# A fused attention and mixture-of-experts layer on one core: a third row buffer, a reordered DMA queue, one group's statistics moved to ScalarE, and three first chunks turned by DMA

## Time and profile before

| | |
|---|---|
| median of 3 runs (lowest, highest) | 440.42 us (439.35, 440.53) |
| the profiled execution | 441.75 us |
| its span, first to last instruction | 440.0 us |
| TensorE busy | 420.4 us, 96% |
| VectorE, ScalarE, GpSimd busy | 322.4, 222.7, 228.3 us |
| chain that ended last | PE 64%, DVE 13%, DMA 11%, issue 4%, ACT 4% |

### The profile page before, as it was taken

How to read it: one execution, slowest core, us unless ns; L and a number is a source line. 1 busy time by engine, 2 the same in 40 slices (tenths; PEclk the granted TensorE clock), 3 DMA queues, 4 the chain that set the end, 5 groups by cost and what they waited for, 6 DMA issues and landing times.

```text
span 440.0 us, 8367 instructions
## 1 busy us (share of the span) xinstructions
PE 420.4 (96%) x3015; PEld 288.6 (66%) x3015; DVE 322.4 (73%) x838; ACT 222.7 (51%) x444; POOL 228.3 (52%) x353
## 2 busy tenths in 40 slices
PE   6899999998999899999989999999999999999996
PEld 2667576756668676766666666666666666665666
DVE  5989778988888478778747787979796967424553
ACT  3755454452657146545424555545455545454551
POOL 3257851826544826056102566575757576757530
PEclk9999999999999999999999999999999999999999
DMA  7996898366945634266866577676888873234840
GB/s 238 294 294 151 277 295 191 74 130 163 279 90 111 139 115 117 57 216 153 120 96 232 165 245 226 205 250 176 281 156 280 179 206 98 90 120 113 159 98 31
DMA packets 104280, 76.01 MB, mean 173 GB/s; under 512 B 73263, under 2 KB 98108, under 8 KB 102192
## 3 DMA queue, kind: packets, MB, share of 16 engines
q1 hardware_dynamic: 92976, 53.11, 47.3%
q0 software_dynamic: 5824, 16.74, 12.9%
q10 hardware_dynamic: 5440, 5.64, 3.9%
HBM read 31.33 MB, written 28.58 MB: 136 GB/s over the span
## 4 chain that ended last, share of the span: by engine, by line
PE 64%; DVE 13%; DMA 11%; issue 4%; ACT 4%; POOL 1%; SPq 1%; another core or an unknown queue 0%; ACTq 0%; POOLq 0%; DVEq 0%
PE bank L1419 18%; PE bank L1421 18%; PE bank L1420 17%; DMA xg<-in_x 4%; DMA pT<-p_rows 3%; PE bank L1510 3%; DVE sc L1012 3%; PE bank L1513 3%; PE bank L1512 3%; PE bank L1491 2%; ACT sc L1269 2%; DVE p_rows L1033 2%; DMA rows<-xg 1%; DMA slots<-xnr,slot_idx 1%; DMA xeT<-slots 1%
## 5 line engine op out<-in xcount | busy, mean ns | idle before, releaser
L1510 PE MATMUL bank<-v_h,pT 128*128 128x257 f16 x272 | 74.7, 274 | 3.2 <-DMA pT<-p_rows 3.2
L1513 PE MATMUL bank<-v_h,pT 128*128 128x257 f16 x272 | 74.1, 272 | 0.0
L1512 PE MATMUL bank<-v_l,pT 128*128 128x256 f16 x272 | 73.7, 271 | 0.0
L1296 ACT ACTIVATE hid_h<-bank 128x512 f16<-128x512 f32 x64 | 38.1, 596 | 67.7 <-PE bank L1421 59.8
L1102 DVE SCALAR_TENSOR_TENSOR hid_l<-bank,hid_h 128x512 f16<-128x512 f32 x64 | 44.0, 688 | 38.0 <-ACT hid_h L1296 33.7
L1421 PE MATMUL bank<-w_h,hid_l 128*128 128x256 f16 x256 | 69.8, 273 | 0.0
L1419 PE MATMUL bank<-w_h,hid_h 128*128 128x256 f16 x256 | 69.8, 273 | 0.0
L1420 PE MATMUL bank<-w_l,hid_h 128*128 128x256 f16 x256 | 69.8, 273 | 0.0
L1012 DVE CUSTOM_DVE_ANT_0 sc<-bank,bias,score_mul 128x512 f32<-128x512 f32 (+2 forms) x80 | 52.9, 664 | 9.1 <-PE bank L1421 9.0
L1419 PE MATMUL bank<-xT,qT_h 128*128 128x512 f16 (+3 forms) x160 | 55.0, 347 | 3.1 <-DVE cmin L1012 1.7
L1285 ACT ACTIVATE pT<-bank 128x512 f16<-128x512 f32 (+3 forms) x50 | 24.6, 494 | 60.3 <-PE bank L1491 50.9
(11 more groups left out here) (198 smaller groups left out, 919.9 us busy)
## 6 DMA issues: line engine op xcount, KB each, us to landing
raw<-in_w_e SPq DMA_DIRECT2D x5, 2048.0 KB
sc<-in_w_e SPq DMA_DIRECT2D x3, 2048.0 KB
slots<-empty ACTq DMA_DIRECT2D x1, 4224.0 KB, 18.7
gates<-gate SPq DMA_DIRECT2D x8, 512.0 KB
out<-xg SPq DMA_DIRECT2D x7, 512.0 KB
rows<-xg SPq DMA_DIRECT2D x7, 512.0 KB, 7.2
rows<-so SPq DMA_DIRECT2D x7, 512.0 KB
xg<-in_x SPq DMA_DIRECT2D x6, 512.0 KB, 4.4
```

What stands on the lines that cost most here:

```text
L1296: a_.activation(hid_h[:, f % HB, :], sc_ps[f % 2][:, :], ACT.Relu).then_inc(h_hi, 1)
L1510: pe.matmul(pv_ps[t % 2][:, 0:D + 1], p_h, v_h[:, at, q, 0:D + 1], start=kb == 0, stop=False)
L1512: pe.matmul(pv_ps[t % 2][:, 0:D], p_h, v_l[:, at, q, :], start=False, stop=False)
L1513: last = pe.matmul(pv_ps[t % 2][:, 0:D + 1], p_l, v_h[:, at, q, 0:D + 1], start=False, stop=kb == t % NT)
```

## The change

- `p_rows` gets a third buffer, which lies in two rows of `hid_h` (used by the experts alone). `pT_in` becomes one semaphore for each tile parity and chunk, and `high` waits for the chunk three DMA turns back.
- `by_dma`: chunk 0 of tiles 15, 27 and 31 is turned by DMA. Before, tile 15 had chunk 1 turned by DMA, 27 and 31 none.
- In the last tile TensorE's turns stand one step later in the order.
- Group 6's RANK stands at step 1 of tile 23 instead of its last step; group 7's VAL units all stand in tile 23 (before: 23 and 24), its PICK and RANK both in tile 24 (before: 24 and 25).
- Group 3's statistics: VectorE's eight instructions and its variance at step 1 of tile 4 go; ScalarE does, for each of the four tiles, a Copy and a Square with accumulated sums, each waiting for the one before it; GpSimd computes the variance with one more instruction.
- SyncE's queue: turn(4) goes behind the chunk_turns of tile 11, two transposes ahead of `top_out(0)` and two behind it. `next_rows(1)` goes behind the chunk_turn of tile 27.

```diff
-        p_rows = [sb(f"p_rows{k}", [P, GT, 2, P], F16) for k in range(2)]
+        p_rows = [sb(f"p_rows{k}", [P, GT, 2, P], F16) for k in range(NX - 1)]
+        p_rows += [hid_h[:, HB - 2:HB, :].rearrange("p f t -> p (f t)").rearrange("p (b h t) -> p b h t", b=GT, h=2)]
...
-            if t in (REST - 1, TILES - 1):
-                return False
+            if t in (NT - 1, REST - 1, TILES - 1):
+                return c == 0
             if chunks(t) == 4:
-                return c == 1 if t == NT - 1 else c in ((1, 2) if t < NT else (0, 1, 2))
+                return c in ((1, 2) if t < NT else (0, 1, 2))
...
-                mine = [PICK] * first + [RANK] * (last and g != NG + 1)
+                mine = [PICK] * first + [RANK] * (c == 1 if g == LATE - 1 else last and g != NG + 1)
...
-                   REST - 5: [VAL, VAL + 1] * last,
-                   REST - 4: [VAL + 2, VAL + 3] * first + [PICK] * (c == 1),
-                   REST - 3: [RANK] * first,
+                   REST - 5: [VAL, VAL + 1] * first + [VAL + 2, VAL + 3] * last,
+                   REST - 4: [PICK] * first + [RANK] * last,
...
-        STATS_TILE = {4: 3, 8: 4, 11: 5, 13: 6, 14: 7}
+        ROOT_TILES = {(4, 1): [0], (5, 0): [1, 2, 3]}
+        STATS_TILE = {8: 4, 11: 5, 13: 6, 14: 7}
...
                 if t == FIRST_SCALE - 1:
-                    spread(0)
+                    turn(NG, range(2))
+                    top_out(0)
+                    turn(NG, range(2, GT))
+                    top_in(0)
...
                     next_rows(0)
-                    next_rows(1)
-
-            spread(1)
+            next_rows(1)
+
+            top_out(1)
+            top_in(1)
...
+                if g == 3:
+                    pool.wait_ge(square3_made, GT)
+                    step(g_.tensor_scalar(var[1][:, :], mv[1][:, :, 1], 1.0 / D, EPS, ALU.mult, ALU.add))
...
-                    if i >= 2:
-                        act.wait_ge(pT_in[i % 2], i // 2 * 16)
+                    if dma_no(t, c) >= NX:
+                        b, m = in_rows[dma_no(t, c) - NX]
+                        act.wait_ge(pT_in[b % 2][m], landed(b, m))
...
+            def statistics(j):
+                act.wait_ge(x_in[1], 32)
+                act.wait_ge(xn_made, made_to(1))
+                act.wait_ge(square3_made, j)
+                a_.activation(unread[:, :], xg[1][:, j, :], ACT.Copy, scale=1.0 / D, accum_out=mv[1][:, j, 0:1]
+                              ).then_inc(mean3_made, 1)
+                act.wait_ge(mean3_made, j + 1)
+                a_.activation(unread[:, :], xg[1][:, j, :], ACT.Square, bias=mv[1][:, j, 0:1], scale=-1.0,
+                              accum_out=mv[1][:, j, 1:2]).then_inc(square3_made, 1)
...
                         high(t, c)
+                    for q in ROOT_TILES.get((t, c), ()):
+                        statistics(q)
...
-                    if c < chunks(t) and not by_dma(t, c):
-                        turn(t, c)
+                    k = c - 1 if t == TILES - 1 else c
+                    if 0 <= k < chunks(t) and not by_dma(t, k):
+                        turn(t, k)
...
+            turn(TILES - 1, chunks(TILES - 1) - 1)
```

More of the change, by code:

```diff
@@ L280, in layer_kernel @@
         square_made = sem("square_made")
+        mean3_made = sem("mean3_made")
+        square3_made = sem("square3_made")
         xT_hi = sem("xT_hi")
@@ L303, in layer_kernel @@
         pT_lo = sem("pT_lo")
-        pT_in = [sem(f"pT_in{k}") for k in range(2)]
+        pT_in = [[sem(f"pT_in{k}_{c}") for c in range(NG)] for k in range(2)]
         pv_full = sem("pv_full")
@@ L374, in dma_no, with landed @@
             return chunk_no(t, c) - turn_no(t, c)
+        in_rows = [(t, c) for t in range(TILES) for c in range(chunks(t)) if by_dma(t, c)]
+        def landed(t, c):
+            return sum(by_dma(k, c) for k in range(t % 2, t + 1, 2)) * 16
         def chunk_cols(t, c):
@@ L457, in var_to @@
         def var_to(g):
-            return 1 if g == 0 else g + 2
+            return 1 if g == 0 else g + 2 if g < 3 else g + 1
         def tile_rows(g, h):
@@ L492, in _, with top_out, top_in, turn @@
                          ).then_inc(slope_in, 16)
-            def spread(e):
+            def top_out(e):
                 sp.wait_ge(w_maxed, e + 1)
                 sp.dma_start(tops[e, 0:2 * P].rearrange("(p m) -> p m", m=2), wmax[:, :]).then_inc(w_put, 16)
+            def top_in(e):
                 sp.wait_ge(w_put, e * 16 + 16)
                 sp.dma_start(wall[:, :], tops[e, 0:2 * P].partition_broadcast(P)).then_inc(w_spread, 16)
-            def turn(g):
+            def turn(g, tiles=range(GT)):
                 at = key_slot(g // NG, g % NG)
@@ L506, in turn @@
                     sp.wait_ge(score_full, chunk_no(NT, 0))
-                for j in range(GT):
+                for j in tiles:
                     sp.wait_ge(xn_lo, rows_to(g))
@@ L547, in chunk_turn @@
             def chunk_turn(t, c):
[L549 removed]
+                k = dma_no(t, c) % NX
                 sp.wait_ge(pT_lo, chunk_no(t, c) + 1)
@@ L552, in chunk_turn @@
                 sp.dma_start_transpose(pT[:, t % 2, c * GT:c * GT + GT, :, :].rearrange("p b h t -> p (b h) t"),
-                                       p_rows[i % 2][:, :, :, :].rearrange("p b h t -> p (b h t)")
-                                       ).then_inc(pT_in[i % 2], 16)
+                                       p_rows[k][:, :, :, :].rearrange("p b h t -> p (b h t)")
+                                       ).then_inc(pT_in[t % 2][c], 16)
             def next_weights(e):
@@ L586, in _ @@
                 for n in (*SPLIT_TILE, LATE):
-                    if t == {5: 14, LATE: REST - 8}.get(n, SPLIT_TILE.get(n)):
+                    if n != NG and t == {5: 14, LATE: REST - 8}.get(n, SPLIT_TILE.get(n)):
                         turn(n)
                 if t == FIRST_SCALE - 1:
-                    spread(0)
+                    turn(NG, range(2))
+                    top_out(0)
+                    turn(NG, range(2, GT))
+                    top_in(0)
                 if t == SECOND_LOAD:
@@ L684, in inverse @@
             def inverse(g):
-                pool.wait_ge(var_made, var_to(g))
+                if g == 3:
+                    pool.wait_ge(square3_made, GT)
+                    step(g_.tensor_scalar(var[1][:, :], mv[1][:, :, 1], 1.0 / D, EPS, ALU.mult, ALU.add))
+                    settle()
+                else:
+                    pool.wait_ge(var_made, var_to(g))
                 pool.wait_ge(rstd_made, g)
@@ L1496, in values @@
                 if by_dma(t, c):
-                    i = dma_no(t, c)
-                    pe.wait_ge(pT_in[i % 2], i // 2 * 16 + 16)
+                    pe.wait_ge(pT_in[t % 2][c], landed(t, c))
                 else:
```

4 lines of the change are left out of this document (2 added, 2 removed).

## The result

| | before | changed |
|---|---|---|
| median of 9 runs (lowest, highest) | 440.03 us (439.22, 447.26) | 438.18 us (435.02, 438.93) |
| ratio to before, 95% interval | 1 | 0.9951 (0.9928 to 0.9974) |
| the profiled execution | 441.75 us | 438.81 us |
| its span | 440.0 us | 437.1 us |
| TensorE busy | 420.4 us | 420.4 us |

The account below looks back on a forecast made before the run. TensorE, busy 420.4 of 440.0 us, was taken as the bound, its idle times worth what the next wait allows. Terms 0.5 - 0.5 + 0.8 + 0.9 + 0.8 = 2.5 us gave 437.9 us from 440.42, range 435.4 to 440.6.

Parts of the forecast that it names:

- tiles 4 and 5: Statistics moved to ScalarE: the turn of (6, 0) comes at 47.1 instead of 47.61, a gain of 0.5 us.
- tile 11: SyncE's new queue order: the 1.82 us idle time goes but is given back, and the chain lengthens; loss of 0.5 us.
- tile 15: Chunk 0 by DMA instead of chunk 1: values(15, 1) starts at 144.75 instead of 145.52, a gain of 0.8 us.
- tiles 23 to 27: RANK(7) earlier uses 1.05 us of GpSimd's idle time before route(7); less 0.15, a gain of 0.9 us.
- tiles 28 to 31: Third row buffer and tile 31's DMA turn: values(31, 0) waits 0.8 us, so a gain of 0.8 instead of 1.6.
- The rival with the table load: Tiles 4 and 5: Square isn't in the exponential's table, four loads of 1.28 us; slower, 442.5 us; chance 0.05.
- VectorE's statistics of group 6 wait for that load: Tiles 13 and 14: group_in(4)'s load delays VectorE's statistics and the scores behind them, so TensorE gives back 1.8 us.
- the first chunk lands late: Tiles 15, 27 and 31: chunk 0's transpose lands in 4.45 us or more; slower, 442.2 us; chance 0.13.
- It also makes route(6) and its indirect DMAs 0.75 later: Tiles 23 to 27, GpSimd: later RANK(6) delays route(6) by 0.75 us, leaving 1.05 of 1.80 us idle to win.
- slightly later landing: Tile 27: a deduction of 0.15 us from the 1.05 us gain, leaving 0.9.
- only the tail counts: Lateness on GpSimd and in DMAs swallows gains ahead of the experts: 439.6 us, no difference; chance 0.22.
- Tile 12's wait is not given back: Group 6's load comes in time after all, so the 1.82 and the 0.5 count: 435.6 us; chance 0.10.

Follow-up runs that it names:

- later runs: Changed kernel with one part undone each: tile 11's queue 435.31 us, group 3's statistics 437.28, ranks and choice 438.16, tile 15's chunk 437.84, last tile's DMA turn 435.19.
- the three undone parts: Changed kernel with group 3's statistics on VectorE again (0.9967), ranks and choice in their old steps (0.9965), or tile 15's chunk 1 by DMA again (0.9967).
- the unedited kernel of the ninth experiment: The changed kernel run once more with no edit, on the third chip: 436.65 us (435.56 to 440.57), ratio 0.9966 to the kernel before.

## Why the prediction was right, and where it was not

The time (437.9, measured 438.18), the sign and the range held. That the sum came out so well is partly luck, because its terms missed by -0.7, +0.6, +0.1, +0.8 and -0.4 us and cancelled. By its own steps, in us gained; the third column is between the two first profiles, the fourth from undoing the part in the later runs, by the start of the first expert in one profile each:

| part | predicted | first profiles | later runs |
|---|---|---|---|
| tiles 4 and 5 | +0.5 | 0.0, then -0.2 at the ranks at 67.50 | +0.6 |
| tile 11 | -0.5 | +0.1 | -0.9 |
| tile 15 | +0.8 | +0.9 | +1.1 |
| tiles 23 to 27 | +0.9 | +1.7 | +1.0 |
| tiles 28 to 31 | +0.8 | +0.4 | +0.4 (1.4 - 1.0; the 1.4 against the first profile before) |
| sum | +2.5 | +2.9 | +2.2 |

- **Tiles 4 and 5.** The step is right as far as the turn (47.10, predicted 47.1). The step that failed is that the gain ended there, "The turn comes at 47.1 instead of 47.61: gain 0.5", without asking what the unit behind it waits for: in the first profile of the changed kernel the unit at 48.07 waits 0.32 us for a transpose of group 2, where in the kernel before it followed the turn without a wait (47.61 + 0.44), and the whole 0.5 is lost there. In the later runs that wait is not there, and 0.6 stayed. The rival with the table load is out. ScalarE's timeline of the changed kernel has six loads, as before, and none between these two, so Square ran between exponentials:

```profile
15.85 1.28 ACT L1370 ACT_TABLE_LOAD   x1
...
218.14 1.28 ACT L1416 ACT_TABLE_LOAD   x1
```

  The price of about 2.7 us that the Trainium skill (ScalarE: Activation LUTs, section "What ACT_TABLE_LOAD costs") gives for a switch of sets was thus paid nowhere by this change.
- **Tile 11.** That its 1.8 us are given back, and that the new order makes what hangs on the queue later, is shown by undoing it. The step that falls short is "VectorE's statistics of group 6 wait for that load, and in order behind them stand the scores": it names the second of two waits. The first is scale(0, 0), which waits for the maxima to come back. In the kernel before it had no idle time ahead of it; with VectorE ahead of that it became a wait of 1.86 us (2.21 in the later run):

```profile
107.64 0.41 DVE L1073 TENSOR_REDUCE wtop<-gate 128x2 f32<-128x256 f32 x1
```

```profile
107.81 0.42 DVE L1097 TENSOR_REDUCE wtop<-gate 128x2 f32<-128x256 f32 x1 [1.86 <-DMA gate<-tops]
```

  I had those 3.19 us of the earlier trace rows in the chain, but only as what delays the queue. Removing either wait alone gave 0.2 and 0.7, both 2.7. The loss was mis-sized too: 0.9 by undoing it, for 0.5. The first profiles show +0.1 in its place; with one execution of each, and a spread of 0.4 at this point in the later ones, that difference stays open.
- **Tile 15.** Predicted start 143.3 with a wait of 0.84, and 144.75 for the second chunk; measured 143.29 with a wait of 0.55, and 144.74. The rival "the first chunk lands late" is out for this tile, since it took 3.1 us, and in tile 31 it took 3.1 as well. That it landed fast is most of the gain, and the 3.3 us for it were taken over from tile 11: at the 4.45 of the earlier trace rows the same sum gave a loss.
- **Tiles 23 to 27.** The mechanism, RANK(7) earlier and GpSimd's idle time used, was right, and so was the size in the later runs (1.0). In the first profiles the term was too small by 0.8, which can be read off. Tile 15's 0.78 taken out, route(7) starts 1.36 earlier (2.14 - 0.78) for the 1.05 predicted: 0.3. The step behind it that failed is "It also makes route(6) and its indirect DMAs 0.75 later": its last one starts at 196.75 and before at 197.67, with tile 15 taken out 0.14 *earlier*; against that, 0.58 of the 1.80 us idle time remained, behind the late signal told of below. From route(7) to its last scatter GpSimd takes 0.3 less (8.91 against 9.22), the two transfers together change by 0.03, and the 0.15 of "slightly later landing" was not paid. Why GpSimd's own stretch was shorter stays open.
- **Tiles 28 to 31.** The direction is right, and the parts are not. The wait for p_rows went, and with it 1.39 us, more than the whole term. The DMA turn costs 0.98 us, where I had taken it for a gain. The step that failed is the end of it: "TensorE has lost 0.26 + 0.92 of idle time and 0.44 of turn, and could start values(31, 0)" 1.6 earlier. The 0.26 and the 0.92 go with the buffer alone, 1.18 us by the prediction's own numbers, and that is more than the 0.8 it kept; I had priced the two parts together and never the second one against the first. The size, 0.4 for 0.8, is in the landing: counted from the first expert, the transpose goes 206.60 us behind it (422.19 - 215.59), where the sum had 206.04 (427.15 - 221.11), and takes 3.10 us for 3.25.

Of the other rivals, "only the tail counts" (439.6) does not fit: 2.5 of the 2.9 us were won ahead of the experts. "Tile 12's wait is not given back" is refuted by the ledger. The sum of the later runs is not checked by a time: each part stands on one profile, and the ratios of the three undone parts that cost 0.6 to 1.1 us by the trace (0.9965 to 0.9967) are the unedited kernel's; their medians, 437.28 to 438.16 us, do lie above its 436.65, but on another chip.

## What to carry to other kernels

When a wait is removed and the time does not move, list every wait of the engine that TensorE then waits for, in order, with its slack: waits in a row hide one another, and one edit at a time shows each as worth little (0.2 and 0.7 us here) when both are worth 2.7. Price the parts of a change against each other and not only against the kernel before: priced together with the buffer, the DMA turn of the last tile looked like part of a gain, and beside the buffer alone it cost 1 us. A queue's order is judged by its last customer, not its first.

## What the runs showed that I had not expected

**Late signals in the first two profiles.** In the first comparison, before and after, signals of other engines come late in some stretches; the one that the argument meets lies where GpSimd issues indirect DMAs. The matmuls of RANK(7) start up to 195.57, those of the next score at 195.67, and VectorE, idle, reads the ranks at 198.53, its releaser being "remote". GpSimd's last indirect DMA of group 6 starts at 196.75:

```profile
196.75 0.97 POOL L789 DMA_INDIRECT slots<-xnr,slot_idx  x1 [0.30 <-issue]
```

The 2.54 us of the earlier trace rows have the same releaser. Five waits have it in the profile before, four in that of the changed kernel, and none in the twelve later ones. In the unedited kernel of the ninth experiment, with the same DMAs at the same distance, VectorE reads the ranks without idle time:

```profile
194.71 0.19 DVE L1006 COPY counts<-bank 128x40 f32<-128x40 f32 x1
```

What makes the signals late stays open: here the lateness and the DMAs fall together, but the one run that took the DMAs away was made where nothing was late, and whether the chip or the execution makes the difference no run shows. The traces differ in one thing more: the first two hold 4401 and 4531 records of engines' signals, the twelve later ones 5667 to 5753, so what ended a wait is known less well in the first two. The two profiles of this one kernel are 3.05 us apart at the first expert, more than the change itself brought; how much of that is the signals' and how much the transposes' that landed late at 48.07 was not measured.
